# Retention stage of a two-layer kernel: the swapped rotary projection replaced by a VectorE shuffle

## The reference

```python
x = _layernorm(x + _L1_attn_ref(x, ...))
# in it, with 4 heads of 64, dim = ROT_DIM = 32
q, k, v = jnp.split(qkv, 3, axis=-1)
def _rotate_half(t):
    x1 = t[..., 0::2]
    x2 = t[..., 1::2]
    return jnp.stack([-x2, x1], axis=-1).reshape(t.shape)
def apply(x, sc):
    xr, xp = (x[..., :dim], x[..., dim:])
    xr = xr * cos * sc + _rotate_half(xr) * sin * sc
    return jnp.concatenate([xr, xp], axis=-1)
scores = jnp.einsum('bhid,bhjd->bhij', q, k) * decay
ret = jnp.einsum('bhij,bhjd->bhid', scores, v)   # then normalized per head
g = x @ wg.T
mish = g * jnp.tanh(jax.nn.softplus(g))
return mish * y @ wo.T
```

## Time and profile before

| | |
|---|---|
| median of 3 runs | 1465.17 us (1461.19 to 1465.23) |
| profiled execution | 1456.11 us |
| its span, first to last instruction | 1454.4 us |
| PE busy in the span | 82% |
| VectorE busy in the span | 56% |
| mean granted PE clock | 0.89 of full speed |
| retention, from its first projection | 648.53 us |

### The profile page before, as it was taken

One profiled execution on the slowest core, in us unless ns is written; L12 is line 12 of the kernel. 1 busy time (PEld: TensorE's weight loads), 2 busy tenths in 40 slices (PEclk: granted clock), 3 DMA queues, 4 the chain that ended last, 5 costly groups with the idle time before them and its releaser, 6 DMA issues. The chain is left out here.

```text
span 1454.4 us, 19589 instructions
## 1 busy us (share of the span) xinstructions
PE 1185.9 (82%) x6248; PEld 689.2 (47%) x6287; DVE 818.7 (56%) x1572; ACT 520.6 (36%) x1052; POOL 550.8 (38%) x564
## 2 busy tenths in 40 slices
PE   5589999999999699989997515699999997778641
PEld 2242222222222255665455511188888886664321
DVE  6499999999997565333446379712221221114554
ACT  1137777777778432101234100033333332221000
POOL 6002447663536500012110105454444443314775
PEclk9799999999999889989998755589999999888855
DMA  4960531443101400000000100199999999962343
GB/s 133 182 151 8 91 46 21 52 58 45 21 10 16 166 2 1 0 1 1 1 1 1 60 0 1 33 295 303 313 306 305 308 302 231 220 192 57 101 127 97
DMA packets 142584, 154.78 MB, mean 106 GB/s; under 512 B 50674, under 2 KB 111443, under 8 KB 142419
## 3 DMA queue, kind: packets, MB, share of 16 engines
q1 hardware_dynamic: 106882, 98.71, 26.9%
q0 software_dynamic: 12288, 33.57, 9.2%
q10 hardware_dynamic: 23312, 21.24, 4.5%
HBM read 118.34 MB, written 32.51 MB: 104 GB/s over the span
## 5 line engine op out<-in xcount | busy, mean ns | idle before, releaser
L495 ACT ACTIVATE l_ret_store<-attn_st 128x512 f32<-128x512 f32 x512 | 280.0, 598 | 103.5 <-PE attn_st L406 87.3
L519 DVE TENSOR_REDUCE attn_neg<-attn_mx 128x8 f32<-128x1024 f32 x256 | 299.1, 1202 | 13.0 <-PE attn_mx L386 12.1
L1713 DVE COPY exp_y_sb<-exp_y_ps 128x256 f32<-128x256 f32 x160 | 68.0, 425 | 288.7 <-PE exp_y_ps L1658 288.7
L1624 POOL DMA_INDIRECT exp_rows<-x_rows,moe_tok_i x160 | 150.9, 943 | 189.2 <-PE exp_xt_ps L1638 172.6
L1649 PE MATMUL exp_h_ps<-exp_xt,exp_w 128*88 128x128 f32 x1280 | 174.2, 281 | 23.2 <-DMA exp_w<-in_w 22.8
L386 PE MATMUL attn_mx<-attn_k_st,attn_q_st 96*128 96x512 bf16 x512 | 154.9, 384 | 17.8 <-DVE attn_neg L519 15.1
L1658 PE MATMUL exp_y_ps<-exp_w,exp_ht 96*128 96x256 f32 x640 | 167.9, 385 | 0.0
L1649 PEld LDWEIGHTS exp_h_ps<-exp_xt,exp_w 128*88 128x88 f32 x1280 | 150.3, 161 | 32.2 <-DMA exp_w<-in_w 31.1
L406 PE MATMUL attn_st<-attn_q_st,attn_k_st 128*128 128x512 bf16 x473 | 160.0, 383 | 5.3 <-ACT l_ret_store L495 2.3
L418 PE MATMUL attn_o<-l_ret_store,l_ret_tab 128*32 128x512 f32 x1024 | 136.4, 604 | 2.8 <-ACT l_ret_store L495 0.8
L1678 ACT ACTIVATE exp_xt<-exp_xt_ps 128x256 f32<-128x256 f32 x160 | 61.5, 384 | 210.4 <-PE exp_xt_ps L1638 206.8
(11 more groups left out here) (233 smaller groups left out, 1643.9 us busy)
## 6 DMA issues: line engine op xcount, KB each, us to landing
exp_w<-in_w SPq DMA_DIRECT2D x320, 176.0 KB
y_rows<-exp_y_sb ACTq DMA_DIRECT2D x160, 128.0 KB, 6.2
parts<-l0b_front SPq DMA_DIRECT2D x32, 192.0 KB, 11.3
attn_k_st<-parts SPq DMA_DIRECT2D x48, 128.0 KB, 7.2
attn_q_st<-parts SPq DMA_DIRECT2D x48, 128.0 KB, 7.9
l_ret_tab<-in_tables SPq DMA_DIRECT2D x4, 1024.0 KB
exp_rows<-x_rows,moe_tok_i POOLq DMA_INDIRECT x160, 6.3
keep_x_t<-in_x_t SPq DMA_DIRECT2D x4, 512.0 KB
```

The source lines that it names most:

```text
L495: act.activation(probs[s % 2][:, h], st_ps[n % BANKS][:], ACT.Exp, scale=SCALE0).then_inc(exp_done, 1)
L519: dve.tensor_reduce(neg[m % 2][:, i], mx_ps[slot["score", n] % 2][:].rearrange("p (j k) -> p j k", k=P), AX.X, ALU.max, negate=True).then_ ...
L1624: pool.indirect_dma_start(rows[b % RB][:], None, a["x_rows"], bass.IndirectOffsetOnAxis(ap=tok_i[:, b:b + 1], axis=0)).then_inc(rows_in[b ...
L1713: dve.tensor_copy(y_sb[b % YB][:], y_ps[b % 2][:, 0:E]).then_inc(y_in, 1)
```

## The change

One projection for each rotation is left. It makes one bank ("rot"), and VectorE makes three operations from it in place of two: a shuffle of partitions within groups of 32, swapping neighbours, from PSUM into sin_part; the cosine product from PSUM; and the sine product, now in place in sin_part. The last one waits for the shuffle to be complete (`rot_read` counts shuffle and cosine product). A bank is free when both have read it. The claims fall from two to one for each rotation, the swapped weights and their two loads go, and the counts that wait for all loads follow from the list's length.

```diff
-RET_W = ("w_k1", "w_ks1", "w_q1", "w_qs1", "w_v1", "w_g1", "w_o1")
-WK, WKS, WQ, WQS, WV, WG, WO = range(len(RET_W))
+RET_W = ("w_k1", "w_q1", "w_v1", "w_g1", "w_o1")
+WK, WQ, WV, WG, WO = range(len(RET_W))
...
         def claim_rot(n):
-            claim("cos", n)
-            claim("sin", n)
+            claim("rot", n)
...
-            return {"cos": (cos_done, n + 1), "sin": (sin_done, n + 1), "v": (v_in, n + 1), "k": (k_in, n + 1),
+            return {"rot": (rot_read, 2 * n + 2), "v": (v_in, n + 1), "k": (k_in, n + 1),
...
-                pool.wait_ge(cos_done, n + 1)
+                pool.wait_ge(rot_read, 2 * n + 2)
                 pool.wait_ge(sin_done, n + 1)
...
-                for kind, i in (("cos", (WQ, WK)[side]), ("sin", (WQS, WKS)[side])):
-                    bank = free_bank(kind, n)
-                    for k in range(KT):
-                        mm = pe.matmul(bank[:], w[:, i, k, m * P:(m + 1) * P], x_t[:, k, c * CH:(c + 1) * CH],
-                                       start=(k == 0), stop=(k == KT - 1))
-                    mm.then_inc(projected, 1)
+                bank = free_bank("rot", n)
+                for k in range(KT):
+                    mm = pe.matmul(bank[:], w[:, (WQ, WK)[side], k, m * P:(m + 1) * P], x_t[:, k, c * CH:(c + 1) * CH],
+                                   start=(k == 0), stop=(k == KT - 1))
+                mm.then_inc(projected, 1)
...
+            swap = [i ^ 1 for i in range(32)]
+
             def rotate(n):
                 c, side, m = rot[n]
                 cc = c % QC
-                dve.wait_ge(projected, 2 * n + 1)
+                bank = a_ps[slot["rot", n] % len(a_ps)]
+                dve.wait_ge(projected, n + 1)
                 if n >= 3:
                     dve.wait_ge(rot_done, n - 2)
-                dve.tensor_tensor(cos_part[:, n % 3], a_ps[slot["cos", n] % len(a_ps)][:],
-                                  tab[:, side, 0, m, cc * CH:(cc + 1) * CH], ALU.mult).then_inc(cos_done, 1)
-                dve.wait_ge(projected, 2 * n + 2)
-                dve.tensor_tensor(sin_part[:, n % 3], a_ps[slot["sin", n] % len(a_ps)][:],
+                dve.stream_shuffle(sin_part[:, n % 3], bank[:], swap).then_inc(rot_read, 1)
+                dve.tensor_tensor(cos_part[:, n % 3], bank[:],
+                                  tab[:, side, 0, m, cc * CH:(cc + 1) * CH], ALU.mult).then_inc(rot_read, 1)
+                dve.wait_ge(rot_read, 2 * n + 2)
+                dve.tensor_tensor(sin_part[:, n % 3], sin_part[:, n % 3],
                                   tab[:, side, 1, m, cc * CH:(cc + 1) * CH], ALU.mult).then_inc(sin_done, 1)
...
-    swap = np.arange(E) ^ 1
-    d["w_qs1"], d["w_ks1"] = (np.ascontiguousarray(d[k][:, swap]) for k in ("w_q1", "w_k1"))
```

## The result

The changed kernel takes 1452.98 us (median of 7, 1447.37 to 1460.89) beside 1465.23 for the kernel before in 7 runs (1461.19 to 1480.38): a ratio of 0.9906, 95% interval 0.9879 to 0.9934. It is faster, by 12.3 us of medians where I had forecast 19.1; 1452.98 lies in my range and 6.9 us above the forecast of 1446.1. The profiled execution took 1450.56 us, 5.6 less than that of before.

The account below looks back on a forecast made before the run. PE was taken to bound retention, with VectorE binding after the change. Gains of 12.92 (first stretch), 2.46 (loop) and 3.72 us (tail) sum to 19.1, so 1465.17 - 19.1 = 1446.1 us, range 1440 to 1457.

Parts of the forecast that it names:

- What bounds it: Retention: PE bounds the first eight rotations and batch 0's loop, at 1.72 us a bank and 3.44 us a rotation.
- The shuffle's price: VectorE, each rotation: priced from the transpose, 0.70 - 0.09 + 0.07 = 0.68 us; bounds 0.60 and 1.30.
- S: Time on VectorE from the shuffle's start to the next operation's start, taken as 0.68 us.
- First stretch: First eight rotations of retention: the bound moves from PE to VectorE, rotations 2.01 us apart, gain 12.9 us.
- Loop and tail: Batch 0's loop: six turns gain 2.46 us; from its last scores to batch 1's first v tile: gain 3.72 us.
- The ring: Loop of batch 0: scores, projection, shuffle, cosine, sine, mask, back to scores make one turn of 5.42 us.
- my own sign: Stated sign of being wrong, in batch 0's loop: PE's clock under 1.00.
- The clock: Rival, batch 0's loop: PE falls to half clock, giving 1467 us, or 1457 for half the loop; chance 0.09.
- GpSimd's exclusion: Rival, first eight rotations: sine product waits for GpSimd's addition, rotations 2.14 us, 0.9 us given back, 1447.0; chance 0.25.
- The two dear shuffles: Rivals, all 16 rotations: shuffle in two passes, 1455.2 us, chance 0.07; slow whatever its size, 1471.7 us, chance 0.02.
- The sum: Whole kernel: 12.92 + 2.46 + 3.72 = 19.1 us saved in retention, all counted at the end, giving 1446.1 us.

Follow-up runs that it names:

- the experiment: Changed kernel ended after retention, plus one extra VectorE product with both inputs in SBUF between shuffle and cosine product of each rotation: 835.63 us.
- the shortened kernels: Kernel before and changed kernel, each ended after retention with the mixture of experts left out and x stored: 836.96 us and 817.88 us.
- the other chip: The whole changed kernel, unaltered, run again on another chip against the kernel before there (1456.47 us): 1433.06 us, ratio 0.9858.
- its two variants: Whole changed kernel with the two swapped-weight loads back, unused: 1439.07 us; and with mask(t + 1) ahead of rotate(8 + t) in batch 0's loop: 1428.03 us.

## Why the prediction was right, and where it was off

*What bounds it.* Right. PE bound the loop before: the order of VectorE's list alone moved one turn of six there, and after the change it was worth 8.7 us. That PE bound the first stretch is read from its rows without a gap, and after the change a second shuffle moved v tile 3 by 4.8 us, eight times 0.6.

*The shuffle's price.* Right: S was forecast as 0.68 and measured as 0.63 (651.78 to 652.41), with 0.73 for the operation and 0.014 for the pattern where I had 0.70 and 0.07. The transpose was a good neighbour. The estimate from the Trainium skill (VectorE: DVE Perf Modes) was 0.80 us for the operation, 0.07 too much; one size can't tell whether the rate or the fixed part is off. A price of 2.4 us whatever the size is out.

*First stretch.* Right: rotations 1.96 us apart for 2.01, gain 32.29 - 19.21 = 13.1 us for 12.9.

*Loop and tail.* The mechanism right, the size off. The ring is 5.35 us for 5.42, but six turns took 717.69 - 683.97 = 33.72 us, not 32.52: one turn lost 1.6 us to the clock. By my own sign, a clock under 1.00 in the loop, that turn was forecast wrong. The gain was 1.3 us for 2.46. In the tail I charged four PE blocks their shortest steps; it took 7.34 us for 7.05, a gain of 3.4 for 3.7.

*The rivals.* The clock was one of them, at 0.09, for the loop as a whole or half of it. It came, but in one turn of six in four profiles (the one with the loads back among them) and three of six in one, at 1.6 us each, and not for good. I had argued against it that no pause was over 1.6 us; the pause of the first turn is 2.14, as its `retain` is shorter than the others (there is no state yet). GpSimd's exclusion exists, as the experiment shows, but costs the changed kernel next to nothing: the sine product of 657.25 starts 0.16 us before the addition's end (656.14 + 1.27) and takes 0.71 us instead of 0.69. If VectorE is let go 0.12 us before that end, as in the experiment, hardly anything is left of the overlap. I gave it 0.25 and 0.9 us. The two dear shuffles are out.

*The sum.* For retention it was right: 19.1 us forecast, 17.9 in the profiles (the pieces above are 13.1 + 1.3 + 3.4); most of what is missing is the turn that the clock lengthened. That the shortened kernels' medians lie just 19.1 apart is luck to the tenth: 1.2 us of it lies ahead of retention in their profiles. The step that did not hold on the first chip is the sentence before the prices: "I count a microsecond taken from retention as one taken from the end". There 12.3 us of 19.1 arrived (interval 9.7 to 17.7, which leaves 19.1 out), on the other chip 23.4 (14.1 to 27.2). The table puts the difference into experts and combining, which change by up to 11 and 12 us between the profiles. For combining, the changed kernel's own second profile has neither the 12 to 14 us waits nor the longer stage, so they don't come with the change every time; the experts took 363.8 and 363.0 us in both, but 352.6 and 360.1 in its two variants and 360.2 and 360.8 before. The two ratio intervals (0.9879 to 0.9934 and 0.9813 to 0.9903) overlap from 0.9879 to 0.9903, which is 14 to 18 us of gain. I take it that the gain arrives and the rest is scatter; the 7 runs, whose interval is 0.55% wide, can't tell a loss of 2 us from one of 9. This is argued. Not shown is that the later stages lose nothing at all by starting earlier: a loss of a few microseconds would hide in the same scatter. What holds the engines in the combining stage was not tried and stays open, as does the source of the experts' spread.

## What to carry to other kernels

When work moves off the engine that binds, write down the ring that binds next and see what in it is only an order: here the mask stood behind a rotation for no need, and that one line was worth 8.7 us more in the shortened kernel (5.0 by the medians of the whole one), but only after the change. An engine that gets pauses can lose its clock, so price the first, longest pause and not the average one. And where late stages scatter by more than the effect, measure a kernel cut off behind the change.

## What the runs showed of the hardware

A shuffle of 128x512 f32 from PSUM takes 0.726 us, 0.03 more than a product of that size, and its pattern load 0.014 us. A VectorE product with both inputs in SBUF stands while a GpSimd addition that began before it runs: 0.67 us became 1.40. A pause of PE of 2.14 us behind a short turn was followed by the 1.2 GHz level for most of one projection, 3.5 to 3.6 us in place of 1.98, in all five profiles of the changed kernel, whole or shortened. Pauses of 1.06 to 1.15 us were followed by it in 2 of 25 turns of these profiles, pauses of 1.75 to 1.79 us in 3 of 8 (the kernels with a second shuffle or an extra product), and pauses of 2.74 and 2.76 us both times.
